# Two norms move to ScalarE, a time-step series becomes a scan, the B and C taps leave TensorE, and a sum moves to GpSimd

## The chip, the cores and the metric

The kernel runs on one core of one Trainium2 chip. The metric is the device time of one execution in microseconds (us), as the median over runs. The core has TensorE (PE), VectorE (DVE), ScalarE (ACT), GpSimd (POOL) and the queues that start DMAs; SyncE (SP) issues the direct ones, GpSimd the indirect ones.

## The reference

Three layers are computed for 32 sequences of 256 rows. Cut to what matters here:

```python
# 1. tokenizer: 9-tap convolution 64 -> 128, scaled by the norm of its window, tanh, relu  (32, 248, 128)
# 2. mamba2 on it, after a layer norm:
zxbcdt = x @ in_proj_w                      # z 256 | x 256 | B 64 | C 64 | dt 4
xBC = silu(depthwise_conv4(x|B|C) + conv_b) # causal, 4 taps along time
dt = softplus(dt + dt_bias);  decay = exp(dt * A)
h = decay * h + dtx * B;  y = h . C         # per head
y = (y + D * xh) * silu(z)
y = y * rsqrt(mean(y * y) + EPS) * norm_w   # mean over 256 channels, two halves of 128
out = y @ out_proj_w                        # and the residual
# 3. layer norm, router over 16 experts (top 2), shared expert, expert layers, mixture,
#    layer norm, last feed-forward layer
```

The recurrence is done in quadratic form: a scan builds the decays between any two rows of a sequence, and the scores C.B are multiplied by them.

## The kernel before

The work falls into stages. A setup stage loads and folds weights (to about 30 us). The main stage (about 30 to 655 us) computes everything up to the routing. Then come 139 blocks of expert work (to about 955 us) and the last feed-forward layer.

The change lies in the main stage and the weight folding ahead of it. The main stage handles 16 units of two sequences (496 columns, or 4 blocks of 124 rows) in 22 steps, a software pipeline written out by hand. In step t unit a = t has its tokenizer convolution and first layer norm, unit b = t-1 its projections and time steps, unit c = t-2 the scores, scans and output projection, unit d = t-3 the second layer norm, router logits and shared expert. Each engine has a list of its own for a step, and runs it in order; semaphores (`S.x_ready`) tie the lists together. The convolution of x, B and C is folded into the weights: each tap is a product of its own, and each fp32 product is three matmuls (high by high, low by high, high by low part; lines 623 to 625), so a chunk with taps takes 12 matmuls of 496 columns and one without takes 3.

Names that come up below. On PE: `dt_projection`, `projection(b, k)`, `x_rows` (L706, waits for ScalarE's silu of the second x chunk), `shared_up` (L802), `mix(c, n)` (L751 and L753), `output` (L761, waits for `S.yg_ready`, and its second part L768, row sums of the squares, for `S.sq_summed`), `shared_down` (L817) and `hn_transposes` (L657), the last of a step. On GpSimd: `rs8_of` (L1030, the two inverse roots of the second norm), the indirect DMAs that scatter rows to `x_slots` (L1043), `exp_of` (L997), `add_bias` (L990), `gate(c, n)` (L1020), `decay_of` (L1008 to L1012), `rstd_of` (L1001, L1002), `rr_of` (L1026). On ScalarE: `square(c, n)` (L928), `silu` (L915 to L921), `residual_input` (L959). On DVE: `norm` (L1104), `normed` (L1224), `dt_rest` (L1123 to L1135), `skip_add` (L1178), `sum_squares` (L1185), `new_stats` (to L1215), `choose` and `slots` of the routing, which are in every second step from t = 5 on. From t = 5 GpSimd also has eight scatters in each step.

## Time and profile before

| | us |
|---|---|
| median of 3 runs | 1109.75 |
| lowest and highest | 1108.16, 1110.27 |
| the profiled execution | 1112.74 |
| its span in the profile | 1111.0 |
| PE busy | 948.3 (85%) |
| DVE busy | 746.7 (67%) |
| POOL busy | 572.2 (51%) |
| ACT busy | 441.8 (40%) |

Busy shares are averages over all stages. A matmul row shows its whole passage through the array, so neighbours overlap; how long a group of matmuls holds PE is read from the start of one row to the start of the next. Brackets at the end of a row of the timeline give the idle time ahead of it and the instruction that ended it.

### The profile page before, as it was taken

To read this page: it belongs to the slowest core of one execution; us is meant where nothing else is said; L and a number is where in the kernel's file an instruction comes from. 1 tells how busy PE (TensorE), PEld (TensorE's weight loads), DVE (VectorE), ACT (ScalarE), POOL (GpSimd) and SP (SyncE) were. 2 spreads that over 40 slices of the span, in tenths; PEclk is the share of its full clock that TensorE was granted. 3 is DMA by queue.
4 is the path that set the end of the run, shared out by engine and by line. 5 is a ranking of instruction groups with operands and counts; after the bars stand their busy time and mean duration, and the time that the engine had idled before them with its cause. 6 is when DMAs were issued, how large, how long until landed. Compare 5 with 4: busy or idle time off the path is not lost. (4 is left out here: it accounts for less than half of the span.)

```text
span 1111.0 us, 22688 instructions
## 1 busy us (share of the span) xinstructions
PE 948.3 (85%) x6371; PEld 795.0 (72%) x6372; DVE 746.7 (67%) x2288; ACT 441.8 (40%) x1068; POOL 572.2 (51%) x531
## 2 busy tenths in 40 slices
PE   0499999999999999999887429999999999388887
PEld 0377877877777777778665229999999999266665
DVE  4348779788797797978866615555555555488884
ACT  3233443343433333423322215555555555144443
POOL 3044444665676556775655735555555555243342
PEclk9899999999999999999986659999999999699999
DMA  6400000000000000000036422222222221223331
GB/s 134 104 20 10 1 10 11 29 20 22 17 29 29 22 24 12 29 20 17 12 95 201 137 69 61 55 63 60 63 66 62 66 62 49 74 56 91 92 92 37
DMA packets 71868, 58.97 MB, mean 53 GB/s; under 512 B 18992, under 2 KB 61291, under 8 KB 71808
## 3 DMA queue, kind: packets, MB, share of 16 engines
q1 hardware_dynamic: 63264, 41.88, 14.4%
q0 software_dynamic: 8544, 16.34, 4.4%
q8 instruction: 32, 0.52, 0.2%
q14 instruction: 28, 0.23, 0.1%
HBM read 35.62 MB, written 23.81 MB: 53 GB/s over the span
## 5 line engine op out<-in xcount | busy, mean ns | idle before, releaser
L1429 POOL DMA_INDIRECT y_tokens<-arena x139 | 155.9, 1122 | 144.7 <-DVE arena L1452 111.3
L1416 ACT ACTIVATE arena<-psum,arena 128x128 f32<-128x128 f32 x556 | 158.6, 368 | 132.0 <-PE psum L1390 130.8
L1390 PE MATMUL psum<-arena 128*128 128x128 f32 x1112 | 155.9, 284 | 3.5 <-DVE arena L1447 1.2
L1390 PEld LDWEIGHTS psum<-arena 128*128 128x128 f32 x1112 | 137.1, 194 | 16.2 <-issue 8.3
L1403 PE MATMUL psum<-arena 128*128 x1112 | 147.8, 275 | 0.4 <-ACT arena L1416 0.4
L1043 POOL DMA_INDIRECT x_slots<-arena,idx x128 | 127.3, 994 | 35.9 <-issue 35.9
L1444 DVE COPY arena<-arena 128x644 f32 x139 | 69.3, 499 | 109.5 <-DVE arena L1452 89.8
L1403 PEld LDWEIGHTS psum<-arena 128*128 128x128 f32 x1112 | 136.0, 193 | 0.6 <-issue 0.6
L623 PE MATMUL psum<-hnT_hi,w_tap_hi 128*128 128x496 f32 x192 | 80.3, 418 | 0.0
L1152 DVE TENSOR_TENSOR_SCAN arena<-psum,arena 124x496 f32<-124x496 f32 x64 | 72.4, 1173 | 6.7 <-PE psum L736 6.7
L624 PE MATMUL psum<-hnT_lo,w_tap_hi 128*128 128x496 f32 x192 | 75.8, 395 | 0.0
L625 PE MATMUL psum<-hnT_hi,w_tap_lo 128*128 128x496 f32 x192 | 75.3, 392 | 0.0
L1452 DVE TENSOR_TENSOR arena<-psum,arena 128x128 f32<-128x128 f32 x139 | 40.6, 292 | 40.2 <-PE psum L1403 38.3
L1603 ACT ACTIVATE arena<-psum,b_f 128x496 f32<-128x496 f32 x64 | 43.1, 673 | 58.0 <-PE psum L1584 58.0
L1020 POOL TENSOR_TENSOR arena<-arena 128x496 f32<-128x496 f32 x32 | 40.8, 1274 | 42.8 <-DVE arena L1178 42.8
L1494 POOL TENSOR_TENSOR rs<-ve,minus_half 124x4 f32<-124x4 f32 x16 | 16.3, 1018 | 88.9 <-DVE ve L1536 88.9
L1576 PE MATMUL psum<-w_f,arena 128*124 128x128 f32 x512 | 59.6, 275 | 1.1 <-ACT arena L1603 0.8
L1542 DVE TENSOR_SCALAR arena<-arena,mv,rs 124x128 f32<-124x128 f32 x64 | 48.3, 813 | 18.1 <-POOL rs L1494 18.1
L1576 PEld LDWEIGHTS psum<-w_f,arena 128*124 128x124 f32 x512 | 57.1, 187 | 4.6 <-issue 3.0
L1447 DVE TENSOR_SCALAR arena<-psum,lng,lnb 128x128 f32<-128x128 f32 x139 | 56.4, 406 | 5.4 <-PE psum L1397 5.4
L997 POOL TENSOR_TENSOR arena<-euler,arena 124x16 f32<-124x16 f32 x16 | 47.8, 2987 | 20.9 <-DVE arena L1118 20.8
L1584 PE MATMUL psum<-arena,w_f 128*128 128x496 f32 x128 | 57.5, 593 | 0.9 <-ACT arena L1594 0.9
(249 smaller groups left out, 2051.2 us busy)
## 6 DMA issues: line engine op xcount, KB each, us to landing
arena<-x_slots SPq DMA_DIRECT2D x139, 64.5 KB
arena<-y_tokens SPq DMA_DIRECT2D x16, 448.0 KB
arena<-in_x SPq DMA_DIRECT2D x16, 256.0 KB, 2.9
out_tokens<-arena SPq DMA_DIRECT2D x16, 224.0 KB
arena<-in_ew SPq DMA_DIRECT2D x1, 2304.0 KB
y_tokens<-arena POOLq DMA_INDIRECT x139
x_slots<-zero_src SPq DMA_DIRECT2D x33, 64.5 KB, 2.7
arena<-in_x SPq DMA_DIRECT2D x4, 512.0 KB, 6.7
```

Of the source, the lines that this page charges most:

```text
L623: nc.tensor.matmul(o, stationary[0], moving[0], start=start, stop=False)
L624: nc.tensor.matmul(o, stationary[0], moving[1], start=False, stop=False)
L625: return nc.tensor.matmul(o, stationary[1], moving[0], start=False, stop=stop)
L1043: nc.gpsimd.indirect_dma_start(out=x_slots, out_offset=bass.IndirectOffsetOnAxis(ap=idx[g % 2][:, col:col + 1], axis=0), in_=x_st[u % NXS] ...
L1152: V.tensor_tensor_scan(L0.rearrange("p h t -> p (h t)")[:, g * 2 * L:(g + 1) * 2 * L], psum[0:CH, 5 + g, 0:2 * L], diag2.rearrange("p h t ...
L1390: last = nc.tensor.matmul(psum[:, 2 + b.q % 2, k * 128:(k + 1) * 128], w1_blk[b.q % 4][:, k * 128:(k + 1) * 128], hT[b.q % 2], start=True, ...
L1403: last = nc.tensor.matmul(psum[:, 4 + c.q % 2, 0:F], EHT[c.q % 2][:, k * 128:(k + 1) * 128], w2[:, ds(at + k * F, F)], start=(k == 0), sto ...
L1416: last = nc.scalar.activation(EHT[t.q % 2][:, k * 128:(k + 1) * 128], psum[:, 2 + t.q % 2, k * 128:(k + 1) * 128], ACT.Silu, bias=w1_blk[t ...
L1429: nc.gpsimd.indirect_dma_start(out=y_tokens, out_offset=bass.IndirectOffsetOnAxis(ap=xb[t.q][:, F:F + 1].bitcast(i32), axis=0), in_=YO[t.q ...
L1444: nc.vector.tensor_copy(w1_blk[t.q % 4], w1[:, ds(at, EW)]).then_inc(X.w1_ready, 1)
L1576: last = nc.tensor.matmul(psum[0:CH, 5, j * F:(j + 1) * F], FH[:, k, j * CH:(j + 1) * CH], w_f2[:, k, :], start=(k == 0), stop=(k == NF - 1))
L1584: nc.tensor.matmul(psum[:, 1 + k, 0:UT], w_f1[:, k * 128:(k + 1) * 128], fhT, start=True, stop=True).then_inc(D.up_psum, 1)
```

## The change

`norm` and `normed` leave DVE. ScalarE computes both as scale times x plus bias, with the biases (minus mean times inverse root) made by small GpSimd instructions that are added to `rstd_of` and `rs8_of`; `rs8_of` also takes over the two small results that DVE made for `residual_input`. `dt_rest` replaces a chain of Horner steps by one scan over 8 coefficients for each of 16 values. B and C are projected without taps (`bc_projection`, 3 matmuls in place of 12), and first in the step; ScalarE makes the last tap with the bias (`bc_begin`), DVE adds the other three (`bc_taps`), and ScalarE takes the silu (`bc_silu`). The order of the other chunks becomes x, x, z, z. `sum_squares` moves to GpSimd. The arena's buffers shift.

```diff
-        chunks = (("z", 0, 3), ("x", 0, 2), ("x", 1, 2), ("z", 1, 3), ("bc", 2, 3))
+        chunks = (("x", 0, 2), ("x", 1, 2), ("z", 0, 3), ("z", 1, 3))
...
+                def bc_projection(b):
+                    later(pe, S.ip_used, 4 * b)
+                    product(psum[:, 3, 0:UT], [v[:, 512:640] for v in w_in2],
+                            [v[:, :, PADL:] for v in hnT2[b % 2]], True, True).then_inc(S.bc_psum, 1)
...
+                def bc_begin(b):
+                    act.wait_ge(S.bc_psum, b + 1)
+                    later(act, S.bct_ready, b)
+                    nc.scalar.activation(bc_sum.rearrange("p b t -> p (b t)"), psum[:, 3, 0:UT], ACT.Identity,
+                                         scale=cw_bc[:, KC - 1:KC], bias=cb[:, 2:3]).then_inc(S.bc_begun, 1)
...
+                def bc_silu(b):
+                    act.wait_ge(S.bc_used, b + 1)
+                    i = bc_sum.rearrange("p b t -> p (b t)")
+                    nc.scalar.activation(BT[b % 2], i[0:64, :], ACT.Silu)
+                    nc.scalar.activation(CT[b % 2], i[64:128, :], ACT.Silu).then_inc(S.bct_ready, 1)
...
+                def norm(a):
+                    act.wait_ge(S.rstd_ready, a + 1)
+                    later(act, S.hnT_psum, a)
+                    for j in range(4):
+                        last = nc.scalar.activation(hn[:, j, :], Hb[:, 4 * F * a + j * F:4 * F * a + (j + 1) * F],
+                                                    ACT.Identity, scale=rstd[:, j:j + 1], bias=nmn[:, j:j + 1])
+                    last.then_inc(S.hn_ready, 1)
...
+                    if b is not None: bc_begin(b)
+                    if a is not None: x_copy(a)
+                    if d is not None: normed(d)
                     if b is not None: silu(b, 0)
-                    if a is not None: x_copy(a)
-                    if b is not None: silu(b, 1)
                     if d is not None: stage(d)
+                    if b is not None: bc_silu(b)
...
+                def sum_squares(c):
+                    pool.wait_ge(S.sq_ready, 2 * c + 2)
+                    nc.gpsimd.tensor_tensor(Sq[:, 0, :], Sq[:, 0, :], Sq[:, 1, :], ALU.add).then_inc(S.sq_summed, 1)
...
                 def rs8_of(c):
                     pool.wait_ge(S.ve8_ready, c + 1)
-                    nc.gpsimd.tensor_tensor(rs8[:, :], ve8[:, :], minus_half[0:CH, 0:8], ALU.pow)\
+                    later(pool, S.xst_ready, c)
+                    g = slice(4 * c, 4 * c + 4)
+                    nc.gpsimd.tensor_scalar(neg8[:, :], MV[:, g, 0], -1.0, 0.0, ALU.mult, ALU.add)
+                    link(pool, S.pool_link, nc.gpsimd.tensor_tensor(rs8[:, :], ve8[:, :], minus_half[0:CH, 0:8],
+                                                                    ALU.pow))
+                    nc.gpsimd.tensor_tensor(nm2[:, :], neg8[:, :], rs8[:, 4:8], ALU.mult)
+                    nc.gpsimd.tensor_tensor(nmr[:, g], neg8[:, :], rs8[:, 0:4], ALU.mult)
+                    nc.gpsimd.tensor_scalar(r1p[:, g], rs8[:, 0:4], 1.0, 1.0, ALU.mult, ALU.add)\
                         .then_inc(S.rs8_ready, 1)
...
+                def bc_taps(b):
+                    dve.wait_ge(S.bc_begun, b + 1)
+                    u = psum[:, 3, 0:UT].rearrange("p (b t) -> p b t", b=2)
+                    for back in range(1, KC):
+                        o = bc_sum[:, :, back:]
+                        last = V.scalar_tensor_tensor(o, u[:, :, 0:L - back], cw_bc[:, KC - 1 - back:KC - back], o,
+                                                      ALU.mult, ALU.add)
...
                     if c is not None: scans(c, 0)
                     if b is not None: dt_first(b)
                     if a is not None: x_rest(a)
                     if c is not None: decayed_scores(c, 0)
-                    if d is not None: normed(d)
+                    if b is not None: bc_taps(b)
                     if m is not None: choose(m)
                     if b is not None: dt_rest(b)
```

On GpSimd, from the end of one steady step to the middle of the next (the indirect DMAs, which follow the second norm's small work and stand around the row with euler, are not among these rows). Before:

```order
L1026 TENSOR_TENSOR arena<-arena,minus_half 124x4
L1030 TENSOR_TENSOR rs<-ve,minus_half 124x8
L997 TENSOR_TENSOR arena<-euler,arena 124x16
L990 TENSOR_TENSOR arena<-arena,tokb 124x512
L1020 TENSOR_TENSOR arena<-arena 128x2x248
L1008 TENSOR_TENSOR arena<-arena,a_neg 124x16
```

The same stretch of the changed kernel, from `gate(c, 1)` on:

```order
L1063 TENSOR_TENSOR arena<-arena 128x2x248
L1069 TENSOR_TENSOR arena<-arena 128x496
L1073 TENSOR_TENSOR arena<-arena,minus_half 124x4
L1079 TENSOR_SCALAR neg<-MV 124x4
L1080 TENSOR_TENSOR rs<-ve,minus_half 124x8
L1082 TENSOR_TENSOR nm<-neg,rs 124x4
L1083 TENSOR_TENSOR nmr<-neg,rs 124x4
L1084 TENSOR_SCALAR r1p<-rs 124x4
L1037 TENSOR_TENSOR arena<-euler,arena 124x16
L1030 TENSOR_TENSOR arena<-arena,tokb 124x512
```

The sum of the squares' halves (L1069) has come in behind the gate, one small row ahead of the inverse roots and three behind them, all ahead of the scatters.

On ScalarE, the first part of a steady step, up to the tanh. Before:

```order
L915 ACTIVATE arena<-psum 128x496
L881 ACTIVATE xT_hi<-psum 128x512
L917 ACTIVATE arena<-psum,cb 128x496
L942 ACTIVATE arena<-row_ids 124x8
L944 ACTIVATE arena<-arena 124x4x128
L887 ACTIVATE arena<-psum 128x496
L935 ACTIVATE arena<-psum,lnb,lng 128x496
L893 ACTIVATE arena<-psum,scale 124x128 x4
```

And in the changed kernel:

```order
L952 ACTIVATE arena<-psum,cb,cw_bc 128x496
L892 ACTIVATE xT_hi<-psum 128x512
L925 ACTIVATE arena<-Hb,nm,rs 124x128 x4
L946 ACTIVATE arena<-psum,cb 128x496
L979 ACTIVATE arena<-row_ids 124x8
L981 ACTIVATE arena<-arena 124x4x128
L958 ACTIVATE arena<-arena 64x496
L959 ACTIVATE arena<-arena 64x496
L898 ACTIVATE arena<-psum 128x496
L972 ACTIVATE arena<-psum,lnb,lng 128x496
L904 ACTIVATE arena<-psum,scale 124x128 x4
```

The second norm (L925) and the two silus of B and C (L958, L959) now stand ahead of the copy of the convolution (L887 before, L898 now).

On PE, from the end of `mix(c, 1)` to the end of the step in the changed kernel; before, twelve matmuls with taps stood where L631 to L633 stand:

```order
L762 MATMUL psum<-arena 64x248
L764 MATMUL psum<-arena 64x124
L631 MATMUL psum<-hnT_hi,w_in_hi 128x496
L632 MATMUL psum<-hnT_lo,w_in_hi 128x496
L633 MATMUL psum<-hnT_hi,w_in_lo 128x496
L772 MATMUL psum<-arena 124x128 x8
L779 MATMUL psum<-ones_col,arena 124x1 x4
L828 MATMUL psum<-w_s,arena 124x128 x8
L665 MATMUL psum<-ident,arena 128x124 x4
```

The slot between the mix and the output projection is the only one on PE that gets shorter: the two other chunks that changed places are as long as before in their slots.

## Rows read from the trace of the kernel before

**Rows 1.** Four steps: length, busy PE, PEld, DVE, ACT, POOL (counts); clock, DMA share, GB/s
```profile
134.62:166.25 31.63, 31.35 (x204) 25.56 (x203) 25.23 (x79) 12.90 (x25) 13.96 (x11) 1.00 0.03 9
...
372.57:406.50 33.93, 31.86 (x213) 26.05 (x212) 30.54 (x99) 12.58 (x25) 21.89 (x19) 1.00 0.08 24
406.50:440.13 33.63, 31.32 (x203) 25.54 (x202) 25.35 (x79) 12.68 (x25) 21.89 (x19) 1.00 0.08 24
...
474.07:509.30 35.23, 32.95 (x204) 26.66 (x203) 25.35 (x79) 12.69 (x25) 21.88 (x19) 0.95 0.05 16
```

**Rows 2.** Timeline of PE in step 12: start, us, instruction, count, idle before
```profile
406.50 0.59 PE L657 MATMUL psum<-ident,arena 124*128 124x124 f32 x4
...
428.56 1.09 PE L706 MATMUL psum<-ident,arena 128*124 128x128 f32 x8 [2.12 <-ACT arena L917]
...
435.54 1.91 PE L761 MATMUL psum<-arena 128*124 128x128 f32 x16
437.42 1.03 PE L768 MATMUL psum<-ones_col,arena 128*124 128x1 f32 x8
...
440.13 0.59 PE L657 MATMUL psum<-ident,arena 124*128 124x124 f32 x4
```

**Rows 3.** Timeline of GpSimd in the same step
```profile
409.99 1.64 POOL L1030 TENSOR_TENSOR rs<-ve,minus_half 124x8 f32<-124x8 f32 x1 [3.90 <-DVE ve L1215]
411.80 1.06 POOL L1043 DMA_INDIRECT x_slots<-arena,idx  x1 [0.17 <-issue]
...
416.69 3.02 POOL L997 TENSOR_TENSOR arena<-euler,arena 124x16 f32<-124x16 f32 x1
...
426.04 1.25 POOL L1020 TENSOR_TENSOR arena<-arena 128x496 f32<-128x496 f32 x1
...
430.56 0.22 POOL L1012 TENSOR_TENSOR arena<-arena,keep 124x16 f32<-124x16 f32 x1
430.74 0.20 POOL L1001 TENSOR_TENSOR arena<-arena,eps_row 124x4 f32<-124x4 f32 x1
...
433.75 1.30 POOL L1020 TENSOR_TENSOR arena<-arena 128x496 f32<-128x496 f32 x1 [1.73 <-DVE arena L1178]
```

**Rows 4.** Timeline of ScalarE in the same step
```profile
427.33 0.62 ACT L928 ACTIVATE arena<-arena 128x496 f32<-128x496 f32 x1 [0.56 <-POOL arena L1020]
427.85 0.66 ACT L917 ACTIVATE arena<-psum,cb 128x496 f32<-128x496 f32 x1
...
435.08 0.62 ACT L928 ACTIVATE arena<-arena 128x496 f32<-128x496 f32 x1 [3.06 <-POOL arena L1020]
...
437.12 1.65 ACT L959 ACTIVATE Hb<-Hb,nmr,r1p 124x128 f32<-124x128 f32 x4
```

**Rows 5.** Timeline of DVE in the same step
```profile
415.20 0.66 DVE L1169 TENSOR_TENSOR arena<-arena,psum 124x496 f32<-124x496 f32 x1
...
432.82 0.86 DVE L1178 SCALAR_TENSOR_TENSOR arena<-arena,d_col,psum 128x248 f32<-128x248 f32 x2 [2.74 <-PE psum L753]
```

**Rows 6.** Timeline of PE: the same wait in step 11 and in step 10
```profile
394.60 1.09 PE L706 MATMUL psum<-ident,arena 128*124 128x128 f32 x8 [1.55 <-ACT arena L917]
...
359.32 1.85 PE L706 MATMUL psum<-ident,arena 128*124 128x128 f32 x8 [2.08 <-ACT arena L917]
```

**Rows 7.** Timeline of PE: first of twelve matmuls of the B and C chunk, and what follows
```profile
329.57 0.49 PE L623 MATMUL psum<-hnT_hi,w_tap_hi 128*128 128x496 f32 x1
...
332.38 1.91 PE L761 MATMUL psum<-arena 128*124 128x128 f32 x16
```

**Rows 8.** One line: small tensor_scalar of GpSimd in the setup, ns min/median/max
```profile
L458 POOL TENSOR_SCALAR a_neg<-a_neg x4: 223/398/777, 22.7 to 24.2; 124x4 f32<-124x4 f32 x4
```

**Rows 9.** Timeline: a fold of the setup, the first norm, and PE in steps 16 and 17
```profile
28.18 1.75 DVE L531 TENSOR_TENSOR w_tap_lo<-arena,w_tap_hi 128x1536 fp32r<-128x1536 f32 x1
...
48.44 1.11 DVE L1104 TENSOR_SCALAR arena<-Hb,arena 124x128 f32<-124x128 f32 x4 [1.42 <-POOL arena L1002]
...
553.10 0.64 PE L783 MATMUL psum<-ident,arena 124*128 124x124 f32 x4 [2.79 <-DVE arena L1224]
...
586.57 1.09 PE L783 MATMUL psum<-ident,arena 124*128 124x124 f32 x4 [7.14 <-DVE arena L1224]
```

More of the change, by code:

```diff
@@ L239, in audio_tower @@
         w_in = take(F, 644)
-        w_tap = take(F, KC, 384)
+        w_tap = take(F, KC, 256)
         tokw = take(128, 5, F)
@@ L269, in audio_tower @@
         ss = take(CH, 16)
-        s2 = take(CH, 16)
-        pa = rq
-        pb = take(CH, 16)
-        tt = pb
+        tt = take(CH, 16)
+        factor = take(CH, 16, NK)
+        coef = take(CH, 16, NK)
+        series = take(CH, 16, NK)
         dA = nab
@@ L298, in audio_tower @@
         hhT = take(128, UT)
+        bc_sum = take(128, 2, L)
         SH = take(128, 2, UT)
@@ L854, in _ @@
                     if d is not None: logits(d)
-                    if b is not None: projection(b, 2, None); projection(b, 3, None); x_rows(b)
+                    if b is not None: projection(b, 1, None); projection(b, 2, None); x_rows(b)
                     if d is not None: shared_up(d, b)
@@ L858, in _ @@
                     if c is not None: mix(c, 1)
[L859 removed]
+                    if b is not None: projection(b, 3, d)
                     if c is not None: output(c)
@@ L899, in relu, with normed @@
                     nc.scalar.activation(Hb[:, rows_of(a)], v_b, ACT.Relu).then_inc(S.h_ready, 1)
+                def norm(a):
[5 more added lines that the diff above has]
+                    last.then_inc(S.hn_ready, 1)
+                def normed(d):
+                    act.wait_ge(S.rs8_ready, d + 1)
+                    if d >= NXS:
+                        act.wait_ge(scattered[d % NXS], 128 * (d // NXS))
+                    for j in range(4):
+                        last = nc.scalar.activation(x_st[d % NXS][0:CH, j, 0, 0:F],
+                                                    Hb[:, 4 * F * d + j * F:4 * F * d + (j + 1) * F],
+                                                    ACT.Identity, scale=rs8[:, 4 + j:5 + j], bias=nm2[:, j:j + 1])
+                    last.then_inc(S.xst_ready, 1)
                 def hnT_copy(a):
                     act.wait_ge(S.hnT_psum, a + 1)
-                    later(act, S.ip_ready, 5 * (a - 1))
+                    later(act, S.ip_ready, 4 * (a - 1))
                     nc.scalar.activation(hnT2[a % 2][0][:, :, PADL:],
@@ L971, in _ @@
                     if c is not None: square(c, 0)
-                    if b is not None: silu(b, 2); silu(b, 3)
+                    if b is not None: silu(b, 1); silu(b, 2)
                     if d is not None: shared_silu(d)
+                    if a is not None: norm(a)
                     if c is not None: square(c, 1)
-                    if b is not None: silu(b, 4)
+                    if b is not None: silu(b, 3)
                     if d is not None: residual_input(d)
@@ L1056, in _ @@
                     if a is not None: rstd_of(a)
-                    if c is not None: gate(c, 1)
+                    if c is not None: gate(c, 1); sum_squares(c)
                     if c == UNITS - 1: scatter(UNITS - 4, (0, 1))
@@ L1098, in stats @@
                     last.then_inc(S.stats_ready, 1)
-                def norm(a):
-                    dve.wait_ge(S.rstd_ready, a + 1)
-                    later(dve, S.hnT_psum, a)
-                    for j in range(4):
-                        last = V.tensor_scalar(hn[:, j, :], Hb[:, 4 * F * a + j * F:4 * F * a + (j + 1) * F],
-                                               mv[:, j, 0:1], rstd[:, j:j + 1], ALU.subtract, ALU.mult)
-                    last.then_inc(S.hn_ready, 1)
                 def dt_first(b):
@@ L1216, in new_stats @@
                         .then_inc(S.ve8_ready, 1)
-                def normed(d):
-                    dve.wait_ge(S.rs8_ready, d + 1)
-                    if d >= NXS:
-                        dve.wait_ge(scattered[d % NXS], 128 * (d // NXS))
-                    for j in range(4):
-                        last = V.tensor_scalar(x_st[d % NXS][0:CH, j, 0, 0:F],
-                                               Hb[:, 4 * F * d + j * F:4 * F * d + (j + 1) * F],
-                                               MV[:, 4 * d + j, 0:1], rs8[:, 4 + j:5 + j],
-                                               ALU.subtract, ALU.mult)
-                    last.then_inc(S.xst_ready, 1)
-                    V.tensor_scalar(r1p[:, 4 * d:4 * d + 4], rs8[:, 0:4], 1.0, None, ALU.add)
-                    V.scalar_tensor_tensor(nmr[:, 4 * d:4 * d + 4], MV[:, 4 * d:4 * d + 4, 0], -1.0, rs8[:, 0:4],
-                                           ALU.mult, ALU.mult).then_inc(S.aff_ready, 1)
                 def logits(d):
@@ L1289, in slots @@
                     V.tensor_copy(idx[m % 2][0:CH, 0:2 * n], slot_f[:, 0:2 * n]).then_inc(S.idx_ready, 1)
+                V.memset(factor[:, :, 0:1], 0.0)
+                for k in range(NK):
+                    V.memset(coef[:, :, k:k + 1], 1.0 / ((2 * (NK - 1 - k) + 1) * 4 ** (NK - 1 - k)))
                 for q in range(NXS):
@@ L1314, in _ @@
                     if c is not None: skip_add(c, 1)
-                    if a is not None: norm(a)
                     if b is not None: x_scale(b)
-                    if c is not None: sum_squares(c); mean_squares(c); residual(c)
+                    if c is not None: mean_squares(c); residual(c)
                     if d is not None: shared_out(d)
```

90 lines of the change are left out of this document (45 added, 45 removed).

## The prediction

> **What bounds the kernel now.** I first read the busy shares: PE 85%, so the first guess is that fewer matmuls make it faster. The change touches only the main stage, so I cut that into its steps (one from each start of L657 to the next) and read each apart. PE shows some 31.3 to 31.9 us of busy time in a step of 33.6 to 33.9 us, DVE 25 or 31, GpSimd 22, ScalarE 13 [rows 1]. So PE is nearly full, but not quite, and the question is what ends its waits.
>
> In step 12 PE has one large wait: 2.12 us ahead of `x_rows` (L706) [rows 2]. Its releaser, the silu L917 on ScalarE, stands behind the square L928, which waited for GpSimd's gate L1020 [rows 4]. On GpSimd that gate is the end of a chain without a hole: it begins with L1030 at 409.99, when DVE's `new_stats` is done, and runs through four scatters, `exp_of`, four scatters and `add_bias` to the gate, which starts at 426.04 and ends near 427.3 [rows 3]. So the ring that sets the step is: row sums of squares (L768), inverse root, residual and `new_stats` on DVE, L1030, 17.3 us of GpSimd, square, silu, `x_rows`, `shared_up`, `mix`, `skip_add`, gate, output, L768 again. PE is full on one part of the ring and waits on the other. A cross-check: step 4 has no scatters (11 GpSimd instructions in place of 19), and takes 31.63 us against 33.63 [rows 1].
>
> What I carry from this: work taken from PE ahead of `x_rows` only makes that wait longer; work added on GpSimd between L1030 and the gate lengthens the step one for one; only what lies between `x_rows` and L768 can give something back.
>
> **The change part by part.**
>
> *B and C without taps.* Twelve matmuls hold PE from 329.57 to 332.38, 2.81 us or 0.234 each [rows 7]. Nine go, 2.1 us a step and some 33 us in 16 steps, if PE alone set the step. The slot that shrinks is the last one, between `mix(c, 1)` and `output`, from 2.81 to 0.7 us. But under it lies another chain. With X = 428.56, the start of `x_rows`: `skip_add` starts at X+4.26 [rows 5], the gate at X+5.19 and ends at X+6.49 [rows 3], and the output L761 starts at X+6.98 [rows 2]. So the twelve matmuls hid that chain all but 0.43 us, and the output will now start near X+6.55: gain 0.43, and 1.6 us of new waiting.
>
> *Sum of squares on GpSimd.* Square: 435.08 to 435.70 [rows 4]; then a GpSimd sum of 496 columns, nearest row the gate of the same size, 1.25 to 1.30 [rows 3]: done at 437.0, PE goes on at X+8.5. Now L768 starts at X+8.86 in this step [rows 2]. So of the 0.43, some 0.33 is left. Steps with routing are 0.30 longer (33.93 against 33.63 [rows 1]); there DVE comes late with this sum, and that goes too.
>
> *GpSimd's small work for the norms.* In `rs8_of`: one tensor_scalar ahead of L1030, a wait for it, three small ones behind, all ahead of the first scatter. The nearest rows are L1012 to L1001, 0.18 from start to start [rows 3]; four of them and 0.1 for the wait make 0.85 us. Lower bound 0.5 (some overlap). Upper bound 1.6: the same form in the setup has a median of 0.398 [rows 8], beside busy DVE, which it is here as well. I take 0.85, nearer to the rows of this stage. This is on the ring, every step. The additions in `rstd_of` (about 0.5) lie ahead of the second gate, which waits 1.73 us for DVE anyway [rows 3]: free.
>
> *ScalarE.* Both norms add 1.65 us each by the same form, L959 [rows 4]. `normed` starts when `rs8_of` ends, near 412.5, and is over by 414.2; its reader on PE comes about 417.7, so it is hidden. `bc_silu` waits for DVE's taps: these start where `normed` did, behind L1169 (415.20) [rows 5], and take three times about 0.7 (half of that form's 496 columns, 0.86 for two, by L1178 [rows 5]): 417.9. The two silus put the copy of the convolution at 419.2, 1.3 us later than now, and PE's transposes of it 0.2 us later; that only fills the wait at `x_rows`. `norm` on ScalarE ends about 1 us ahead of the second square: hidden. If it weren't, the square, L768 and the whole ring would move with it.
>
> *DVE.* Two norms, one sum and half the Horner chain leave, three taps come. DVE waits in each of these steps now (2.74 us in this one [rows 5]), so nothing on the ring gets shorter by it, except the 0.30 above.
>
> *The ring in all.* 33.63 - 0.33 + 0.85 = 34.15 us, with routing or without. Steps 5 to 15 are 11: six with routing at +0.22, five without at +0.52: +3.9 us. Steps 2 to 4, without scatters, have PE as the bound up to the output: about -0.15 each, -0.5.
>
> *Clock.* In step 10 the wait of 2.08 us was followed by L706 at 1.85 in place of 1.09 us [rows 6], the granted clock of such a step is 0.95 and it takes 35.23 in place of 33.63 [rows 1]; three of the eleven steps are so. After 1.55 us it never fell [rows 6]. The waits at `x_rows` grow to about 2.2 with routing and 2.8 without. I take three more falls at 1.35 us (1.6 less what the neighbours give back): +4.1; bounds none and eight more.
>
> *Start.* The weight fold is a third smaller: of 1.75 us [rows 9] 0.55 goes, and as much in the folds before it, less one more small DMA: -0.6. In steps 0 and 1 PE waits for `norm`: ScalarE's 1.65 against DVE's 1.11 [rows 9] and 0.5 on GpSimd: +1.05 twice, +2.1.
>
> *Tail.* PE waits 2.79 and 7.14 us for `normed` in steps 16 and 17 [rows 9]; on ScalarE it is early. But then `x_rows` waits for GpSimd (16), and in 17 GpSimd's sum and scatters hold the inverse root: I take -0.8 and -1.6. After that 26 scatters end the stage, behind `rs8_of`: +0.7.
>
> *Sum.* 3.9 - 0.5 + 4.1 - 0.6 + 2.1 - 1.7 = +7.3 us on the profiled execution, 1112.74, so 1120. That execution stands 3.0 us above the median of the runs, 1109.75; from the median it is 1117.
>
> **Rivals.**
>
> *Slower still, by the clock* (0.15). If the longer wait brings the clock down in every step from 5 to 15, it is eight more falls in place of three: 5 x 1.35 = 6.8 us more, 1124. For it: in step 16 the clock also fell, after 2.79 us. Against: most waits of 2.1 us passed.
> The Trainium skill, page "TensorE: Matmul & The Clock Gate", section "HAM oscillation — how this bites in real kernels", describes a kernel in which the wait between bursts of matmuls throttles PE in every turn; no row here shows that for each step, three of eleven do.
>
> *Slower by dear small instructions* (0.10). At 0.4 us each the ring grows by 1.6 in place of 0.85: 11 x 0.75 = 8 more, 1125.
>
> *No change* (0.12). Small instructions at the lower bound, 0.5, and no further falls: 11 steps at about 0 (+0.2 in all), start +1.5, steps 2 to 4 -0.5, tail -1.7: -0.5, 1109.
>
> *Faster* (0.18). The place is the scatter behind L1030. If its preparation, which shows 0.17 us of idle and 0.09 more than a later one, hides the small work, the ring only gains: 11 x -0.47 = -5.2, and with the shorter waits no more falls; -5.9 in all, 1104. It decides where less than 0.4 us of the 0.85 shows up. The far end is PE as the bound after all: 33 us less, 1077; the waits at `x_rows` speak against it, and I give it 0.04 of the 0.18.
>
> **How the numbers follow.** The forecast, a ring longer by 0.2 to 0.5 us and some more falls of the clock, has 0.45: 1112 to 1122. A difference under 0.2% (2.2 us) can't be told from none. Slower 0.45 + 0.15 + 0.10 = 0.70 less 0.02 for its lower edge, 0.68; same 0.12 + 0.02 = 0.14; faster 0.18. The range reaches from the faster case, 1104, to 1126, which takes in both slower rivals and leaves 0.04 below for the far end and some 0.15 at the edges.
>
> **What would show it.** L1069 and four small rows on GpSimd, the first gate about 0.85 us later in its step; the wait at `x_rows` over 2 us in each step; a new wait of about 1.6 us ahead of the output, with GpSimd's gate as its releaser; PE's busy time down by some 30 us and the span not; steps of 34.1 us at full clock. I am wrong if `x_rows` no longer waits for the silu behind the gate, if a step takes under 33.3 us, or if `norm` on ScalarE holds back the second square.

## The result, and the profile after

The changed kernel takes 1118.26 us (median of 7 runs, 1116.68 to 1122.34) against 1109.75 for the kernel before (7 runs, 1108.16 to 1113.96): a ratio of 1.008, 95% interval 1.006 to 1.010. It is slower. Its profiled execution took 1121.03 us, with a span of 1119.2.

From the page of the changed kernel: busy time of each engine, and the group of its costly ones that the page of before did not have.

```profile
PE 928.0 (83%) x6227; PEld 775.4 (69%) x6228; DVE 706.2 (63%) x2057; ACT 498.4 (45%) x1212; POOL 606.3 (54%) x643
...
L772 PE MATMUL psum<-arena 128*124 128x128 f32 x256 | 35.0, 294 | 25.0 <-POOL arena L1063 25.0
```

PE and DVE have 20 and 40 us less to do, ScalarE and GpSimd 57 and 34 more, and the time went up by 8. The second line says where PE's saving went: over all steps PE now stands 25.0 us ahead of the output projection, for GpSimd's gate, where the twelve matmuls used to stand.

Seven steps by windows, the answer to [rows 1] (from the start of L665 to the next: steps 2, 3, 4, 12, 13, 14 and 15):

```profile
75.97:108.00 32.03, 29.30 (x161) 24.67 (x161) 19.72 (x44) 11.00 (x22) 12.69 (x12) 0.84 0.03 9
108.00:143.41 35.41, 33.92 (x194) 27.88 (x195) 23.18 (x67) 16.63 (x34) 17.15 (x19) 0.86 0.03 8
143.41:174.74 31.33, 29.58 (x194) 23.77 (x193) 22.83 (x64) 16.47 (x34) 16.07 (x18) 1.00 0.04 9
413.58:447.64 34.06, 29.57 (x194) 23.79 (x193) 22.78 (x64) 16.24 (x34) 23.98 (x26) 1.00 0.08 24
447.64:481.72 34.08, 30.13 (x204) 24.35 (x203) 28.15 (x84) 16.24 (x34) 24.06 (x26) 1.00 0.08 24
481.72:518.62 36.90, 32.41 (x194) 25.25 (x193) 22.78 (x64) 16.13 (x34) 23.99 (x26) 0.91 0.05 15
518.62:554.22 35.60, 31.64 (x204) 25.47 (x202) 28.14 (x84) 16.12 (x34) 24.11 (x26) 0.95 0.05 15
```

A step at full clock takes 34.08 with routing (13) and 34.06 without (12), where it was 33.93 and 33.63. PE's busy time in it fell from 31.9 to 30.1 and from 31.3 to 29.6, and none of that shows in its length.

PE in step 12, the answer to [rows 2]:

```profile
413.58 0.59 PE L665 MATMUL psum<-ident,arena 124*128 124x124 f32 x4
...
436.49 1.09 PE L717 MATMUL psum<-ident,arena 128*124 128x128 f32 x8 [2.83 <-ACT arena L946]
442.97 2.01 PE L772 MATMUL psum<-arena 128*124 128x128 f32 x16 [1.40 <-POOL arena L1063]
444.93 1.03 PE L779 MATMUL psum<-ones_col,arena 128*124 128x1 f32 x8
447.64 0.59 PE L665 MATMUL psum<-ident,arena 124*128 124x124 f32 x4
```

`x_rows` (now L717) waits 2.83 in place of 2.12, and the output (L772) waits 1.40 in place of nothing. GpSimd in the same step, the answer to [rows 3]:

```profile
417.10 0.20 POOL L1079 TENSOR_SCALAR neg<-MV 124x4 f32<-124x4 f32 x1 [3.91 <-DVE ve L1264]
...
419.28 0.19 POOL L1084 TENSOR_SCALAR r1p<-rs 124x4 f32<-124x4 f32 x1
419.83 1.07 POOL L1097 DMA_INDIRECT x_slots<-arena,idx  x1 [0.36 <-issue]
...
432.73 1.30 POOL L1030 TENSOR_TENSOR arena<-arena,tokb 124x512 f32<-124x512 f32 x1
433.97 1.25 POOL L1063 TENSOR_TENSOR arena<-arena 128x496 f32<-128x496 f32 x1
441.68 1.24 POOL L1063 TENSOR_TENSOR arena<-arena 128x496 f32<-128x496 f32 x1 [1.28 <-DVE arena L1232]
443.64 1.23 POOL L1069 TENSOR_TENSOR arena<-arena 128x496 f32<-128x496 f32 x1 [0.73 <-ACT arena L965]
```

From the first instruction of `rs8_of` to the first scatter it is 419.83 - 417.10 = 2.73 us, where it was 411.80 - 409.99 = 1.81 [rows 3]: 0.92 more. From there to the gate the chain has no hole: 14.14 us, before 14.24 [rows 3].

Where the 8.2 us of span came from, by the starts of the last transposes (L657 before, L665 after): up to the start of step 2, +2.05; steps 2 and 3, +6.74; step 4, -0.30; steps 5 to 15, 379.48 against 376.98, +2.50; from there to the first block of expert work, 111.80 against 114.41, -2.61; the rest -0.2.

### The profile page after: what moved, and what is told of

It is laid out like the page before. It is cut to its first block and busy times, and to the rows that moved or that the text cites. A ratio compares the mean times of both kernels' runs of the same rounds, so it can differ in the third digit from the quotient of the medians.

```text
span 1119.2 us, 22487 instructions
## 1 busy us (share of the span) xinstructions
PE 928.0 (83%) x6227; PEld 775.4 (69%) x6228; DVE 706.2 (63%) x2057; ACT 498.4 (45%) x1212; POOL 606.3 (54%) x643
## 5 line engine op out<-in xcount | busy, mean ns | idle before, releaser
L1063 POOL TENSOR_TENSOR arena<-arena 128x496 f32<-128x496 f32 x32 | 39.8, 1244 | 31.3 <-DVE arena L1232 31.3
L772 PE MATMUL psum<-arena 128*124 128x128 f32 x256 | 35.0, 294 | 25.0 <-POOL arena L1063 25.0
L1434 PE MATMUL psum<-ident,arena 128*128 128x128 f32 x139 | 38.4, 276 | 20.7 <-DMA arena<-x_slots 20.7
L631 PE MATMUL psum<-hnT_hi,w_tap_hi 128*128 128x496 f32 x128 | 53.9, 421 | 0.0
```

The lines of the kernel that those rows point to most:

```text
L631: nc.tensor.matmul(o, stationary[0], moving[0], start=start, stop=False)
```

## The experiments

Each run is compared with the kernel before on the same chip. Lengths of steps are those at full clock ("clean"), if nothing else is said. On one chip (e1 to e4, and e10 to e12) the kernel before took 1133.5 and 1129.3 us; in the profiles of these seven runs DVE stands 13 to 23 us at the end of the main stage, which no profile of another chip shows. This idle time has another length in each of them, and no profile of the kernel before was taken on that chip. So part of a ratio there can come from it, and these runs are judged by their steps first.

**e0: the changed kernel once more.**

> The changed kernel as it is, as the mark for the other runs, since on another chip the four kernels of the first group all had DVE standing for 17 to 23 us at the end of the main stage, which neither trace shown so far has. The same steps of 34.05 to 34.1 us as in its first trace; ratio to before 1.006 to 1.013. If the stall is there too, it is of the chip and not of the edits.

Measured: 1118.99 us against 1109.46, ratio 1.0092 (1.0057 to 1.0127). Clean steps take 34.04 to 34.11 again, but the clock fell in steps 2, 5, 6 and 7 and not in 3, 14 and 15; steps 5 to 15 come to 379.8 us all the same. In steps 5 to 15 the place where the clock falls is not fixed. In step 2 it fell both times.

**e1: the small work alone.** The kernel before, with four small GpSimd instructions at the place where the change has them, and nobody who reads their results:

```diff
-                    nc.gpsimd.tensor_tensor(rs8[:, :], ve8[:, :], minus_half[0:CH, 0:8], ALU.pow)\
+                    nc.gpsimd.tensor_scalar(neg8, MV[:, g, 0], -1.0, 0.0, ALU.mult, ALU.add)
+                    link(pool, S.pool_link, nc.gpsimd.tensor_tensor(rs8[:, :], ve8[:, :], minus_half[0:CH, 0:8],
+                                                                    ALU.pow))
+                    nc.gpsimd.tensor_tensor(nm2, neg8, rs8[:, 4:8], ALU.mult)
+                    nc.gpsimd.tensor_tensor(nm3, neg8, rs8[:, 0:4], ALU.mult)
+                    nc.gpsimd.tensor_scalar(r1x, rs8[:, 0:4], 1.0, 1.0, ALU.mult, ALU.add)\
                         .then_inc(S.rs8_ready, 1)
```

> The kernel before with nothing changed but rs8_of on GpSimd: one small tensor_scalar ahead of the inverse roots, a wait, and three small instructions behind them (their results go to tiles that nobody reads in this stage). Ring theory: the first scatter starts about 0.9 us later in every step from 5 to 15, and each of these steps is longer by as much, 34.5 to 34.9 us: +10 us, near 1120, with the clock alone adding or taking some 3. Rival (the small work hides, the change is slow by its waits and the clock alone): steps of 33.6 to 33.9, near 1110.

Measured: ratio 1.0112 (1.0075 to 1.0149). Clean steps take 34.55 to 34.60, some 0.65 more with routing and 0.95 more without, as the ring says. GpSimd in one of them:

```profile
455.29 0.19 POOL L1032 TENSOR_SCALAR ve<-MV 124x4 f32<-124x4 f32 x1 [3.92 <-DVE ve L1222]
...
457.47 0.20 POOL L1037 TENSOR_SCALAR mv<-rs 124x4 f32<-124x4 f32 x1
458.03 1.07 POOL L1050 DMA_INDIRECT x_slots<-arena,idx  x1 [0.36 <-issue]
```

It is 2.74 us to the first scatter, as in the changed kernel, and PE's wait at `x_rows` in this step goes to 2.52 (before, 1.55 to 1.61 with routing). So four instructions of 0.2 us, on an engine that is busy half of the time, are enough to lengthen every step with scatters, and by more than the whole change does: the change gives a part back. What they do not explain are steps 2 and 3, which are as long here as before (27.54 and 33.16 us).

**e5: the same work at another place.** As e1, but the four instructions stand behind `rr_of`, where GpSimd then waits 3.9 us for DVE.

```diff
                     nc.gpsimd.tensor_tensor(rr, ms, minus_half[0:CH, 0:4], ALU.pow).then_inc(S.rr_ready, 1)
+                    link(pool, S.pool_link, nc.gpsimd.tensor_scalar(neg8, minus_half[0:CH, 0:4], -1.0, 0.0, ALU.mult, ALU.add))
+                    nc.gpsimd.tensor_tensor(nm2, neg8, minus_half[0:CH, 0:4], ALU.mult)
...
```

> The kernel before with four small GpSimd instructions of the same kinds as in the first experiment, but placed behind rr_of, ahead of the wait for DVE's new statistics (their results go to tiles that nobody reads in this stage). Ring theory: GpSimd waits 3.9 us there, so the steps keep 33.6 and 33.95 us, and the time is that of before within 0.3%. Rival (what costs is the amount of GpSimd's work, or the four instructions beside DVE): as in the first experiment, about +10 us.

Measured: 1110.06 against 1109.46, ratio 1.0006 (0.9985 to 1.0027); clean steps 33.96 and 33.63, as in the kernel before. In its profile the wait ahead of L1035 (`rs8_of`) is shorter by what was added:

```profile
407.20 0.19 POOL L1028 TENSOR_SCALAR ve<-minus_half 124x4 f32<-124x4 f32 x1
...
411.13 1.64 POOL L1035 TENSOR_TENSOR rs<-ve,minus_half 124x8 f32<-124x8 f32 x1 [3.15 <-DVE ve L1220]
412.94 1.07 POOL L1048 DMA_INDIRECT x_slots<-arena,idx  x1 [0.17 <-issue]
```

So it is the place that costs, and not the amount.

**e2: the norms and the residual's two results back on DVE**, the rest as changed (`norm`, `normed`, `rstd_of`, `rs8_of` as in the kernel before; `normed` stands ahead of `bc_taps` on DVE).

> The changed kernel with both norms on DVE and the two small results for the residual there too, as before; B and C taps, the scan and the sum on GpSimd stay. Ring theory: the 0.92 us between the inverse roots and the first scatter go, steps of 33.15 us in place of 34.05 (11 steps, -10 us), and step 0 and 1 get back about 1 us each: 1118.3 - 12, near 1106, faster than before. Rival (ScalarE's new load or the clock makes the kernel slow, not this work): stays above 1114.

Measured: ratio 1.0199 (1.0163 to 1.0235), so the expected 1106 us was missed. Steps without routing are 33.27 to 33.40, shorter than before (33.63), as the ring says. Those with routing take 36.3 to 37.1, none of them at full clock (granted 0.91 to 0.95). PE ahead of `x_rows` (L717) in one of each:

```profile
403.85 1.06 PE L717 MATMUL psum<-ident,arena 128*124 128x128 f32 x8 [2.40 <-DVE arena L1192]
...
508.32 1.09 PE L717 MATMUL psum<-ident,arena 128*124 128x128 f32 x8 [0.80 <-ACT arena L928]
```

With norms, taps and routing in one step DVE's scans (L1192) come last, and the clock falls behind that wait as well; in steps 9 and 13 it fell earlier, behind a wait of 1.26 us. So in this order of work the taps could not have gone to DVE without the move of the norms.

**e3: the B and C taps back on PE** (with them the Horner steps and the old order of chunks), norms and sum as changed:

```diff
-        chunks = (("x", 0, 2), ("x", 1, 2), ("z", 0, 3), ("z", 1, 3))
+        chunks = (("z", 0, 3), ("x", 0, 2), ("x", 1, 2), ("z", 1, 3), ("bc", 2, 3))
```

> The changed kernel with B and C projected with their taps on TensorE again (12 matmuls in the last slot, order z, x, x, z, bc) and the Horner chain in place of the scan; the norms on ScalarE and the sum on GpSimd stay. If PE were the bound, nine more matmuls cost 2.1 us in each of 16 steps: 1118 + 33 = 1151. Ring theory: they refill the wait of 1.4 us ahead of the output and cost 0.4 to 0.7 us a step there: steps of 34.4 to 34.8. If the wait ahead of the output is what lets the clock fall in steps 2 and 3 (7 us lost there), that comes back: between 1116 and 1124. If the clock stays down in steps 2 and 3 without that wait, its cause is elsewhere.

Measured: ratio 1.014 (1.0089 to 1.0192). Clean steps take 34.2 to 34.3, against 34.07 and the expected 34.4 to 34.8: nine matmuls more, 2.1 us of PE [rows 7], cost 0.2 us a step. PE is not the bound. The other question of this run was the clock in steps 2 and 3. Step 3 is at full clock again (32.93 us), but step 2 is not: it takes 33.02 us at 0.84. So its fall does not come from the matmuls that were taken away alone; the part on the prediction comes back to it.

**e4: the sum of the squares back on DVE.**

```diff
-                    if c is not None: gate(c, 1); sum_squares(c)
+                    if c is not None: gate(c, 1)
...
-                    if c is not None: mean_squares(c); residual(c)
+                    if c is not None: sum_squares(c); mean_squares(c); residual(c)
```

> The changed kernel with the sum of the two halves of the squares on DVE again. Ring theory: DVE is idle for 3.3 us there, ends its sum about 0.6 us earlier than GpSimd does, but PE is busy with the output projection until then: the same steps of 34.05 us, 1118 within 1.5. Only in step 17, where GpSimd's sum stands ahead of four scatters, it could give 1 to 2 us. Rival (the sum on GpSimd is on the ring): steps 0.5 us shorter, near 1112.

Measured: ratio 1.0154 (1.0113 to 1.0195), but clean steps of 33.84 to 33.88, 0.2 shorter. From the start of the output to that of the row sums PE now takes 447.36 - 445.51 = 1.85 us, in the changed kernel 444.93 - 442.97 = 1.96.

```profile
445.51 2.01 PE L772 MATMUL psum<-arena 128*124 128x128 f32 x16 [1.39 <-POOL arena L1063]
447.36 0.93 PE L779 MATMUL psum<-ones_col,arena 128*124 128x1 f32 x8
```

So the sum on GpSimd is itself a loss of 0.2 us a step, of which 0.1 shows in these rows, though DVE, its old engine, is the busier one; I had expected no difference. The clock fell in five of the eleven steps here, and still step 15 ends at 553.19, 1.0 us ahead of the changed kernel. What makes the ratio worse than the changed kernel's lies behind that, where DVE stands 19.75 us on this chip; it was not taken apart.

**e6 and e7: the second four scatters later**, in the wait ahead of `rs8_of`; e6 is the changed kernel, e7 the one before:

```diff
-                    if v is not None and v < UNITS - 5: scatter(v, (2, 3))
                     if a is not None: add_bias(a)
...
                     if c is not None: rr_of(c)
+                    if v is not None and v < UNITS - 5: scatter(v, (2, 3))
                     if c is not None: rs8_of(c)
```

> The changed kernel with one edit on GpSimd: the second four scatters of a step stand behind rr_of, ahead of the second norm's work, and not between exp_of and add_bias. Ring theory: 4.9 us leave the chain from the inverse roots to the first gate, the wait at x_rows goes, and PE or, with routing, DVE's scans (ready 20.8 us into the step) become the bound: 31.3 us without and 32.0 us with routing in place of 34.07: -27 us against the changed kernel. Rival (PE, or DVE, or the sum of GpSimd's work is the bound): less than -5 us.

> The same edit in the kernel before. PE then has its full 31.6 and 31.1 us of work and small waits, and DVE's scans with routing: 33.0 and 31.6 us in place of 33.94 and 33.63: -15 us against before. So with GpSimd's chain off the path the change would be worth about 0.3 to 1 us a step, and the order of the two kernels turns round. Rival: if both gain alike, the change is slow for a reason of its own.

Measured: ratios 1.0135 (1.0105 to 1.0165) and 1.0114 (1.0084 to 1.0143); the large gain that I expected did not come. Clean steps take 33.7 and 34.6 us by turns in e6, and 34.2 to 34.4 and 35.0 to 35.2 in e7. So step by step the changed kernel is the shorter one here by 0.5 us, as expected; the ratios do not show it, since e6 stands 5.4 us behind e7 when step 5 starts. GpSimd and PE in e6:

```profile
347.65 0.97 POOL L1097 DMA_INDIRECT x_slots<-arena,idx  x1 [0.30 <-issue]
348.64 0.22 POOL L1079 TENSOR_SCALAR neg<-MV 124x4 f32<-124x4 f32 x1
```

```profile
366.56 1.06 PE L717 MATMUL psum<-ident,arena 128*124 128x128 f32 x8 [2.54 <-DVE arena L1212]
```

Two things went wrong. Four scatters take 5.1 us and the wait that they were to fill takes 3.9, so `rs8_of` starts late: it has no idle time ahead of it now. And `x_rows` waits for DVE's scans (L1212) in place of the silu: a second ring, `rs8_of`, four scatters, `exp_of`, DVE's time-step chain, scans, `x_rows`, that the first one had covered. Steps 5 to 15 of e6 still come to 376.9 us, as long as before (377.0); it loses its time ahead of step 5 (5.8 us) and behind step 15 (3.9 us).

**e10, e11, e12: all eight scatters in one turn**, `exp_of` straight behind `rs8_of`; e10 is the changed kernel, e11 the one before, e12 is e10 with the sum on DVE.

```diff
-                    if v is not None and v < UNITS - 5: scatter(v, (2, 3))
+                    if v is not None and v < UNITS - 5: scatter(v, (0, 1))
...
                     if a is not None: rstd_of(a)
+                    if v is not None and v < UNITS - 5: scatter(v, (2,))
...
+                    if v is not None and v < UNITS - 5: scatter(v, (3,))
                     if c is not None: rs8_of(c)
-                    if u is not None and u < UNITS - 5: scatter(u, (0, 1))
```

> The changed kernel, with all eight scatters of a chunk issued in one turn of GpSimd's loop: the first four behind exp_of (where (2, 3) of the chunk before stood), two behind rstd_of, two behind rr_of; none between rs8_of and exp_of. Theory: GpSimd's stretch from rs8_of to the first gate is the ring that sets the step, and the second ring of the earlier test (rs8_of, scatters, exp_of, DVE's scans, x_rows) is relieved too, since exp_of stands directly behind rs8_of. Then the ring is some 5 us shorter, and PE sets the steps without routing (near 31.7 us; the shorter taps pay here), DVE the steps with routing (near 32.6): against 34.07 in the changed kernel some 21 us less in all, 1098 (1092 to 1106). Rival: two scatters at 1.27 us each do not fit ahead of rs8_of or the second gate, rs8_of is late again, and it stays at 1115 to 1125.

> The kernel before, with the same order of scatters. PE's busy time in a step is 31.3 to 31.9 us there and it becomes the bound: near 32.0 us without routing, DVE near 33.0 with it, against 33.63 and 33.93: 1093 (1086 to 1101). If PE is what sets the step then, e10 has the shorter steps without routing (nine matmuls, 2.1 us, less, of which the output wait gives some 1.4 back); if e10 is slower still, the added GpSimd and DVE work weighs more than the matmuls even with the ring relieved. Rival: as for e10, rs8_of late, 1115 to 1122.

> As e10, and the sum of the two halves of the squares back on DVE. With the sum on GpSimd, GpSimd ends its turn later and PE's output was stretched by 0.2 us; with it on DVE, the steps without routing are 0.2 us shorter than in e10, and those with routing 0.3 to 0.6 longer if DVE sets them (+2 us in all), shorter by 0.2 if it does not (-2 us).

Measured: 1.0186 (1.0147 to 1.0224), 1.0009 (0.9982 to 1.0037) and 1.0228 (1.0187 to 1.0268). All three expectations were missed. The first reasons are again in GpSimd's rows. In e10:

```profile
406.32 1.27 POOL L1063 TENSOR_TENSOR arena<-arena 128x496 f32<-128x496 f32 x1 [1.87 <-DVE arena L1233]
...
414.62 1.07 POOL L1097 DMA_INDIRECT x_slots<-arena,idx  x1 [0.16 <-issue]
416.00 0.97 POOL L1097 DMA_INDIRECT x_slots<-arena,idx  x1 [0.30 <-issue]
416.98 1.25 POOL L1063 TENSOR_TENSOR arena<-arena 128x496 f32<-128x496 f32 x1
...
427.95 0.19 POOL L1079 TENSOR_SCALAR neg<-MV 124x4 f32<-124x4 f32 x1 [1.39 <-DVE ve L1265]
```

The pair ahead of the second gate does not fit there: gate to gate is 10.66 us, in the changed kernel 441.68 - 433.97 = 7.71, and output, sum, `rr_of` and `rs8_of` all move with it. No step from 5 on is at full clock. Those without routing take 34.2 and 34.3 us at 0.95 (one took 36.7 at 0.87): the output waits 2.82 us for the gate there, and the clock falls behind that wait. Those with routing take 37.0 to 38.7. In e11 the steps without routing come down to 32.3 to 32.6 (from 33.63; one took 33.3), and those with routing go up to 35.8: there DVE has no idle time from 442.11 to 466.5 and `x_rows` waits 2.15 for its scans. The two cancel, which is the ratio of 1.0009. e12's steps without routing were no shorter than e10's (34.2 to 34.3, also at 0.95), so the 0.2 that e4 gave back does not show where the second gate is what is late.

**e13: one pair of scatters where it fits**, in the changed kernel: `scatter(v, (3,))` alone ahead of `rs8_of` (2.6 us in a wait of 3.9), `scatter(u, (0,))` ahead of `exp_of`, `scatter(v, (1, 2))` behind it.

> The changed kernel, and only one pair of each chunk's eight scatters moved to where GpSimd has room: the last pair stands between rr_of and rs8_of, in the wait of 3.91 us (two scatters take 2.6), and one pair is left between rs8_of and exp_of, two pairs between exp_of and add_bias. Nothing is added ahead of the second gate, rr_of or rs8_of that does not fit. Theory of the ring: its stretch on GpSimd from rs8_of to the first gate is two scatters, 2.6 us, shorter, so x_rows waits 0 to 0.3 us in place of 2.3 to 2.8 and a step takes 31.7 us without routing (PE) to 32.6 with it (DVE), with no falls of the clock behind x_rows: 11 steps by about 1.9 us, 1097 to 1101 from 1118, that is a ratio of about 0.990 (0.984 to 1.000) to the kernel before. Theory of the second ring (exp_of, DVE's time-step chain, scans, x_rows): exp_of now starts 2.6 us earlier behind rs8_of too, so it does not bind either. Rival: the room ahead of rs8_of is not there once the ring is shorter (DVE's row sums, residual and new_stats come at the same time, rs8_of waits for the scatters), and the step stays above 33.5: ratio 1.005 or more.

Measured: 1116.09 against 1109.33, ratio 1.0053 (1.0032 to 1.0073). Half of the expectation came true to a tenth: steps without routing take 31.61 to 31.63 us (31.90 in step 6). Those with routing take 35.9 to 36.1 (37.9 in step 15), expected 32.6; none of them is at full clock. Windows of one of each:

```profile
411.90:443.53 31.63, 29.51 (x194) 23.76 (x193) 22.88 (x64) 16.22 (x34) 24.24 (x27) 1.00 0.08 26
443.53:479.60 36.07, 31.73 (x203) 24.82 (x202) 29.96 (x84) 16.25 (x34) 24.24 (x27) 0.95 0.07 23
```

DVE's busy time in the second is 29.96 us, in the changed kernel's step with routing 28.15, with the same 84 instructions. One of them has all of the 1.8 us. DVE in a step without and in one with routing, and GpSimd's addition beside the second:

```profile
424.24 0.27 DVE L1173 TENSOR_TENSOR arena<-arena 124x112 f32<-124x112 f32 x1
...
459.54 2.08 DVE L1173 TENSOR_TENSOR arena<-arena 124x112 f32<-124x112 f32 x1
```

```profile
460.19 1.29 POOL L1030 TENSOR_TENSOR arena<-arena,tokb 124x512 f32<-124x512 f32 x1
```

```profile
432.37 1.09 PE L717 MATMUL psum<-ident,arena 128*124 128x128 f32 x8 [0.41 <-ACT arena L946]
...
466.83 1.06 PE L717 MATMUL psum<-ident,arena 128*124 128x128 f32 x8 [2.66 <-DVE arena L1213]
```

So the ring through GpSimd is gone (the wait at `x_rows` for the silu is 0.41), and in steps with routing DVE is what comes last: it works without a hole from 444.82 to the scans (L1213), 1.8 us of it in one instruction that stands still beside GpSimd's `add_bias`. The wait of 2.66 us that follows also brings the clock down, 0.95 in this window. All five steps with routing from 7 to 15 show the 2.1 us. Without these 1.8 us and the some 1.6 us that a fall costs, such a step would take about 32.6 us, as expected; that is an estimate from the rows. What is left to 31.6 is the routing's own work on DVE (12 instructions, about 3.8 us, part of which fills idle time); it was not tried by itself.

e13's profiled execution is 3.4 us longer than that of the kernel before, and the steady steps are not where that arises: up to the start of step 2 it is +1.0, step 2 (at a granted clock of 0.84) +4.9, steps 3 and 4 -0.6, steps 5 to 15 +0.6, and the rest -2.5.

## Why the prediction was right, and where it was not

The forecast was 1117 us, slower; it is 1118.3. The mechanism held in the steady steps. That the number is so close is partly luck, as the sum below shows. By its steps:

*The ring.* Predicted 34.15 us with or without routing; measured 34.05 to 34.12, and 34.38 in step 6. `rs8_of` was priced at 0.85 and took 0.92; the two ends of that price, 0.5 and 1.6, are settled by the rows of 0.19 to 0.20 us. e1 shows that this work alone lengthens the steps, e5 that the same work off the ring costs nothing. One of the eleven steps is not on this ring: in step 5 GpSimd has no scatters in either kernel, and `x_rows` waits there for DVE's scans (2.13 us before, 1.45 after). That it also takes 34.05 us is chance.

*What comes back between `x_rows` and L779.* The predicted wait ahead of the output was 1.6 us, measured 1.40; L779 starts 8.44 us behind `x_rows`, predicted 8.5, before 8.86 [rows 2]. e3 confirms that the matmuls there had been hiding a chain: with them back a step changes by 0.2 us.

*ScalarE.* `norm` ends at 442.08, 0.86 ahead of the second square (442.94), predicted 1; `normed` is hidden. Right, by the changed kernel's timeline:

```profile
440.43 1.65 ACT L916 ACTIVATE arena<-Hb,nmn,arena 124x128 f32<-124x128 f32 x4 [0.47 <-POOL nmn L1045]
442.94 0.62 ACT L965 ACTIVATE arena<-arena 128x496 f32<-128x496 f32 x1 [0.87 <-POOL arena L1063]
```

*The clock, mis-sized and in the wrong place.* I gave +4.1 us to three more falls in steps 5 to 15. There were two falls there, not six. They cost 4.3 us, the three before 5.1: against 33.93 and 33.63 the three of before stand 1.9, 1.65 and 1.6 us over, the two of after 2.8 and 1.5 over 34.07. Steps 5 to 15 grew by 2.5 us: 3.05 from the longer steps (six by 0.14, five by 0.44), 0.8 less from the falls, and some 0.2 for step 6. So the term that I had at +4.1 is -0.8. The price of a fall was about right, but a longer wait at `x_rows` did not bring more of them: waits of 3.17 us in step 6 and of 2.83 to 2.85 in steps 8, 10 and 12 passed, 2.82 in step 14 and 2.31 in step 15 did not. The prediction's "most waits of 2.1 us passed" is also too favourable: of six such waits in the kernel before (2.08 to 2.21 us) three passed.

*Steps 2 and 3, the term that was missing.* They were to give back 0.15 us each and cost 6.7. PE at the end of step 1 in the kernel before, then from there to the end of step 2 in the changed kernel:

```profile
73.92 0.64 PE L657 MATMUL psum<-ident,arena 124*128 124x124 f32 x4 [0.84 <-DVE arena L1104]
```

```profile
75.97 0.64 PE L665 MATMUL psum<-ident,arena 124*128 124x124 f32 x4 [3.83 <-ACT arena L916]
...
103.60 3.09 PE L772 MATMUL psum<-arena 128*124 128x128 f32 x16 [1.79 <-POOL arena L1063]
108.00 1.07 PE L665 MATMUL psum<-ident,arena 124*128 124x124 f32 x4
```

The wait for `norm` at the end of step 1 was 0.84 us and is 3.83: 2.1 of the difference are the matmuls that no longer stand ahead of it, the rest, 0.9, is the +1.05 that I had priced. As lost time that was right (step 1 is 0.8 longer). But behind it the granted clock goes to half, the lower of its two levels (1.2 GHz), and again behind the new wait of 1.79 for the gate, until about 118:

```profile
76.00:80.00 4.00, 4.00 (x20) 3.57 (x21) 1.12 (x2) 0.96 (x2) 0.00 (x0) 0.63 0.00 0
80.00:84.00 4.00, 4.00 (x18) 3.64 (x18) 3.29 (x8) 0.72 (x1) 0.60 (x1) 0.52 0.00 0
...
108.00:112.00 4.00, 4.00 (x16) 3.29 (x17) 2.66 (x11) 0.58 (x1) 1.02 (x1) 0.50 0.00 0
```

Before, both steps ran at 1.00 (27.53 and 33.17 us). The step of the prediction that failed is this: I asked for the clock only behind `x_rows` in steps 5 to 15, and not behind the other waits that the change makes. e0, where only the first of the two falls came, lost 3.0 us in these two steps.

The first of the two falls is part of the change, and not chance. The clock fell in step 2 in all nine profiles of the kernels that carry the change or most of it (granted 0.84 to 0.89, 30.0 to 33.0 us), and in none of the five that build on the kernel before (wait 0.83 to 0.84, 27.5 us). e2 and e3 take the wait apart. The same wait in e2, with `norm` on DVE and the nine matmuls gone, and in e3, with `norm` on ScalarE and the matmuls back:

```profile
72.97 0.64 PE L665 MATMUL psum<-ident,arena 124*128 124x124 f32 x4 [2.86 <-DVE arena L1129]
```

```profile
76.64 0.64 PE L659 MATMUL psum<-ident,arena 124*128 124x124 f32 x4 [1.80 <-ACT arena L907]
```

That is 2.0 us more than before by the matmuls and 1.0 by the norm, which add up to the 3.0 of the changed kernel; and each of the two alone was enough for the clock to fall (0.89 in e2, 0.84 in e3). The fall in step 3 is not of this kind: the wait of 1.79 us stands in seven profiles, and only two of them, the changed kernel's first and e12, have it.

*Start and tail.* Up to step 2, +2.05, predicted +1.5. The tail gave back 2.6, predicted 1.7: PE's wait for `normed` in step 16 is 0.53 (before 2.79 [rows 9]), and in step 17 it is 5.07 (before 7.14).

The sum, +7.3 predicted and +8.2 measured, so owes its closeness to luck: two errors of opposite sign nearly cancel, 5.5 us too much in steps 5 to 15 and 7.0 too little in steps 2 and 3. The ring does not hang on them: in both profiles of the changed kernel the clean steps are longer by themselves. But of the 8.2 us it makes only some 3; the greater part in this profile is the clock in steps 2 and 3.

*The rivals.* Clock down in every step: refuted, two of eleven. Dear small instructions: refuted, 0.2 us each. Faster because the first scatter's preparation hides the small work: refuted, it shows with its full 0.92, and the preparation grew to 0.36. PE as the bound after all: refuted by e3 for these kernels; only e13's steps without routing, 31.6 us, come near to it, with 0.41 us of waiting at `x_rows` and 1.40 at the output.

What stays open is a version that beats both. e13 takes more off GpSimd's stretch of the ring (two scatters, 2.6 us) than the change had added (0.92), and is still 0.5% slower than the kernel before. DVE then sets every second step, so that steps 5 to 15 together gain nothing, and the fall of the clock in step 2 costs 4.9 us. Moving `add_bias` away from DVE's time-step chain in e13 was not tried, and neither was a shorter wait for `norm` at the end of step 1.

## What to carry to other kernels

In a loop that several engines close in a ring, first find the stretch that has no holes; there 0.9 us of added work cost 0.65 to 0.95 us in every step (e1), on an engine that is busy about half of the time, and 2.1 us taken from the busiest engine gave back 0.2 (e3). When work is taken away, ask which chain it had covered: the new wait of 1.4 us ahead of the output was legible before, from the start of `skip_add` to the end of the gate. A wait that opens on TensorE is to be priced with the clock behind it wherever it opens, in the short steps of a pipeline's start as well as in the steady ones; and two profiles of one kernel, or those of its variants, tell a fall that comes each time from one that does not.

## What the runs showed of the hardware

*DVE standing still beside GpSimd.* In e13 L1173, an fp32 tensor_tensor of 124x112 with both inputs in SBUF, takes 0.27 us, and 2.08 to 2.10 in every step where it falls on GpSimd's `add_bias` (460.19 to 461.48); it ends 0.14 behind that. In e6 the tensor_scalar L1168 (124x16) takes 1.24 us in nine steps in place of 0.17, and ends 0.04 behind the GpSimd addition:

```profile
359.31 1.24 DVE L1168 TENSOR_SCALAR arena<-arena 124x16 f32<-124x16 f32 x1 [3.82 <-POOL arena L1037]
```

```profile
359.25 1.26 POOL L1030 TENSOR_TENSOR arena<-arena,tokb 124x512 f32<-124x512 f32 x1
```

The Trainium skill, page "SBUF — State Buffer", section "SBUF: two separate sides", says that DVE and GpSimd share a pair of ports as a lock: it is taken by a DVE instruction in a two-port mode, or by one with two SBUF inputs beside a GpSimd instruction that reads SBUF, and the one that starts second stands until the first is done. e6's rows agree to 0.04 us, if L1168, which has one input, runs in a two-port mode; no row shows its mode. In e13 DVE's row begins 0.65 us ahead of GpSimd's, so the order of starts alone does not give it. So a change of place on GpSimd, which DVE does not depend on, cost DVE 1.1 us (e6) and 1.8 us (e13).

*DVE standing at the end of a stage on one chip.* In the profiles of e1 to e4 and e10 to e12 DVE stood 13 to 23 us ahead of the last addition of the shared expert (here e4), mostly with a releaser outside the profile, and the kernel before took 2% more on that chip (1129.3 and 1133.5 us) than on the others:

```profile
662.43 0.69 DVE L1278 TENSOR_TENSOR MOE<-psum,b_s 124x512 f32<-124x512 f32 x1 [19.75 <-remote]
```

What it waits for was not found.

*Falls of the clock, some in the same place and some not.* Up to step 15, two profiles of the changed kernel had their falls in steps 2, 3, 14 and 15, and in 2, 5, 6 and 7, with much the same waits: 2.85 us in step 10 passed in the first, and 2.28 in step 7 did not in the second. In step 2 the clock fell in all nine profiles with a longer wait there.
